# Two 3x3 convolutions in three steps: another order of the work on TensorE, ScalarE, VectorE and GpSimd

## What is computed

```python
def _conv(x, w):
    return lax.conv_general_dilated(x, w, window_strides=(1, 1), padding='SAME', ...)
for _ in range(N_STEPS):                       # 3 steps, H_STEP = 1/3
    t = jax.nn.relu(_conv(x, w1) + b1[None, :, None, None])
    x = x + H_STEP * (_conv(t, w2) + b2[None, :, None, None])
return jax.nn.relu(x)
```

## Time and profile before

| | |
|---|---|
| median of 3 runs | 1165.74 us (1165.06 to 1167.67) |
| the profiled execution | 1166.12 us, its span 1164.3 us |
| PE busy | 1078.2 us, 93% |
| DVE busy | 1060.3 us, 91% |
| ACT busy | 653.4 us, 56% |
| POOL busy | 525.9 us, 45% |

### The profile page before, as it was taken

How to read it: one execution, slowest core, us unless ns; L and a number is a source line. 1 busy time by engine, 2 the same in 40 slices (tenths; PEclk the granted TensorE clock), 3 DMA queues, 4 the chain that set the end, 5 groups by cost and what they waited for, 6 DMA issues and landing times. The chain is left out here.

```text
span 1164.3 us, 20990 instructions
## 1 busy us (share of the span) xinstructions
PE 1078.2 (93%) x7238; PEld 604.7 (52%) x7238; DVE 1060.3 (91%) x1481; ACT 653.4 (56%) x1525; POOL 525.9 (45%) x416
## 2 busy tenths in 40 slices
PE   3279999999999999999969999999999999999995
PEld 3167777777777777777633333333333333333331
DVE  5459999999999999999958999999999999999995
ACT  4558888888888888988613232332234232342332
POOL 5134555444554555545323444534435445444440
PEclk9989999999999999999989999999999999999998
DMA  8101111111111111110000000210003000120003
GB/s 304 53 20 28 37 38 29 38 29 37 35 32 29 37 37 33 34 28 20 20 10 1 1 1 1 46 28 1 1 1 73 1 1 1 29 45 1 1 1 73
DMA packets 87544, 35.83 MB, mean 31 GB/s; under 512 B 70209, under 2 KB 86850, under 8 KB 86930
## 3 DMA queue, kind: packets, MB, share of 16 engines
q1 hardware_dynamic: 85634, 33.81, 11.0%
q0 software_dynamic: 768, 0.33, 0.1%
q10 hardware_dynamic: 1040, 0.35, 0.1%
HBM read 26.09 MB, written 8.39 MB: 30 GB/s over the span
## 5 line engine op out<-in xcount | busy, mean ns | idle before, releaser
L1082 PE MATMUL acc<-mixed,cwp 128*128 128x512 f32 x768 | 354.4, 607 | 5.1 <-DVE mixed L1143 2.9
L1082 PEld LDWEIGHTS acc<-mixed,cwp 128*128 128x128 f32 x768 | 139.7, 191 | 218.6 <-issue 214.8
L1100 ACT ACTIVATE y<-acc,cols 128x1024 f32<-128x1024 f32 x96 | 111.6, 1207 | 249.4 <-PE acc L1092 249.4
L1092 PE MATMUL acc<-mixed,cwp 64*64 64x512 f32 x1536 | 184.2, 600 | 11.7 <-POOL mixed L1143 11.5
L842 POOL TENSOR_TENSOR rstd<-var,half 128x8 f32<-128x8 f32 x32 | 80.9, 2527 | 217.6 <-DVE var L733 217.6
L522 DVE TENSOR_TENSOR prod<-qkv 128x1024 f32<-128x1024 f32 x128 | 155.6, 1219 | 7.6 <-POOL qkv L738 7.3
L532 DVE TENSOR_TENSOR prod<-attn,qkv 128x1024 f32<-128x1024 f32 x128 | 155.0, 1235 | 1.1
L1142 POOL TENSOR_TENSOR mixed<-xs 128x256 f32<-128x256 f32 x92 | 83.1, 903 | 156.7 <-DVE xs L1131 156.7
L564 PE MATMUL cb<-consts,prod 128*128 128x128 f32 x1024 | 135.8, 283 | 0.0
L1108 DVE TENSOR_TENSOR y<-y,acc 128x512 f32<-128x512 f32 x192 | 120.5, 678 | 15.9 <-ACT y L1100 15.9
L1116 DVE TENSOR_TENSOR y<-y,acc 128x512 f32<-128x512 f32 x192 | 123.0, 682 | 7.2 <-PE acc L1092 5.2
(11 more groups left out here) (172 smaller groups left out, 1550.1 us busy)
## 6 DMA issues: line engine op xcount, KB each, us to landing
xs<-in_x SPq DMA_DIRECT2D x4, 2048.0 KB, 16.6
xa<-in_x SPq DMA_DIRECT2D x32, 256.0 KB, 2.8
xr<-in_x SPq DMA_DIRECT2D x64, 128.0 KB, 2.9
out_y<-xs SPq DMA_DIRECT2D x32, 256.0 KB, 4.7
cw<-in_L_conv_w POOLq DMA_DIRECT2D x2, 144.0 KB, 4.2
consts<-in_consts ACTq DMA_DIRECT2D x1, 192.0 KB
group<-in_consts SPq DMA_DIRECT2D x1, 64.0 KB
w1n<-in_L_conv_w ACTq DMA_DIRECT2D x1, 64.0 KB
```

Source lines behind the costliest of these rows:

```text
L1082: pe.matmul(psum[PSUM_PAIR[v, q, j]][i][:, :, :], weights(v, i, j).rearrange("p n o -> p (n o)"), mixed[v][i][:, s0:s0 + WIDE, j, :], star ...
L1092: m = pe.matmul(psum[PSUM_PAIR[v, q, j]][i][out, :, :], edge_weights(v, i, j)[rows, :], mixed[v][i][rows, s0 + near:s0 + near + WIDE, j, : ...
L1100: act.activation(pairs(y[i][q][:, :, :]), m1, ACT.Identity, bias=cols[:, (6, 8)[v]:(7, 9)[v]]).then_inc(m1_out[i][q], 1)
```

## The change

It replaces the written order of all four engines by another one with the same pieces. The same pieces stand on the same engines: per iteration DVE makes the 8 outer pieces of x, the 8 outer and 4 inner pieces of h, POOL 8 inner pieces of x and 4 of h. No instruction is added or removed. The iteration's boundaries in the lists lie elsewhere (parts of step g - 1 and g - 2 are now written in round g), which alone changes nothing in the order. The table of PSUM pairs is changed with it. The pieces before the first iteration are as they were.

```diff
         PSUM_PAIR = {
-            (0, 0, 0): 2, (0, 0, 1): 3, (0, 0, 2): 0, (0, 0, 3): 1, (0, 1, 0): 2, (0, 1, 1): 3, (0, 1, 2): 0,
-            (0, 1, 3): 1, (1, 0, 0): 3, (1, 0, 1): 2, (1, 0, 2): 1, (1, 0, 3): 0, (1, 1, 0): 2, (1, 1, 1): 3,
+            (0, 0, 0): 3, (0, 0, 1): 2, (0, 0, 2): 0, (0, 0, 3): 1, (0, 1, 0): 3, (0, 1, 1): 2, (0, 1, 2): 0,
+            (0, 1, 3): 1, (1, 0, 0): 3, (1, 0, 1): 2, (1, 0, 2): 0, (1, 0, 3): 1, (1, 1, 0): 2, (1, 1, 1): 3,
             (1, 1, 2): 0, (1, 1, 3): 1
         }
...
         def dve_iteration(dve, g, steps):
+            if steps[1]:
...
+                dve_sums(dve, g - 1, 1, 0, 1)
+                dve_sums(dve, g - 1, 1, 1, 1)
+                mix_x(dve, g - 1, 0, 1, outer)
+                dve_y(dve, g - 1, 1, 0, 1, 0)
+                dve_y(dve, g - 1, 1, 0, 1, 1)
+                dve_x(dve, g - 1, 0, 1)
+                dve_y(dve, g - 1, 1, 1, 1, 0)
+                dve_y(dve, g - 1, 1, 1, 1, 1)
+                dve_x(dve, g - 1, 1, 1)
...
         def act_iteration(act, g, steps):
...
             if steps[0]:
+                act_m1(act, g, 0, 1, 0)
                 act_m1(act, g, 0, 0, 0)
...
+            if steps[1]:
+                act_result(act, g - 1, 0, 0)
+                act_result(act, g - 1, 1, 0)
+                act_result(act, g - 1, 0, 1)
+                act_result(act, g - 1, 1, 1)
...
-            for g in range(COUNT + 2 - 1):
-                iteration(eng, g, [0 <= g - s < COUNT for s in range(2)])
+            for g in range(COUNT + 3 - 1):
+                iteration(eng, g, [0 <= g - s < COUNT for s in range(3)])
```

More of the change, by code:

```diff
@@ L1204, in pe_iteration @@
[L1204 to L1214, removed]
@@ L1226, in pe_iteration @@
[L1226 to L1229, removed]
-        def act_iteration(act, g, steps):
+        def act_iteration(act, g, steps):
+            if steps[1]:
+                act_hidden(act, g - 1, 0, 1)
+                act_hidden(act, g - 1, 0, 0)
+                act_hidden(act, g - 1, 1, 1)
+                act_hidden(act, g - 1, 1, 0)
+                act_m1(act, g - 1, 0, 0, 1)
+                act_m1(act, g - 1, 0, 1, 1)
+                act_hidden(act, g - 1, 1, 3)
+                act_hidden(act, g - 1, 1, 2)
+                act_hidden(act, g - 1, 0, 2)
+                act_hidden(act, g - 1, 0, 3)
+                act_m1(act, g - 1, 1, 0, 0)
+                act_m1(act, g - 1, 1, 1, 0)
+                act_m1(act, g - 1, 1, 0, 1)
+                act_m1(act, g - 1, 1, 1, 1)
@@ new lines, in dve_iteration @@
+        def dve_iteration(dve, g, steps):
+            if steps[1]:
+                mix_h(dve, g - 1, 0, 0, inner)
+                dve_sums(dve, g - 1, 0, 0, 1)
+                mix_h(dve, g - 1, 1, 0, outer)
+                dve_sums(dve, g - 1, 0, 1, 1)
+                dve_y(dve, g - 1, 0, 1, 1, 1)
+                dve_y(dve, g - 1, 0, 1, 1, 0)
+                dve_y(dve, g - 1, 0, 0, 1, 1)
+                mix_h(dve, g - 1, 1, 1, outer)
+                dve_y(dve, g - 1, 0, 0, 1, 0)
+                mix_h(dve, g - 1, 1, 3, outer)
+                mix_h(dve, g - 1, 0, 2, inner)
+                mix_h(dve, g - 1, 0, 2, outer)
+                mix_h(dve, g - 1, 1, 2, outer)
+                mix_h(dve, g - 1, 0, 3, outer)
+                mix_h(dve, g - 1, 0, 3, inner)
+                dve_sums(dve, g - 1, 1, 0, 0)
+                dve_sums(dve, g - 1, 1, 1, 0)
+                dve_y(dve, g - 1, 1, 0, 0, 1)
+                dve_y(dve, g - 1, 1, 0, 0, 0)
+                dve_x(dve, g - 1, 0, 0)
+                dve_y(dve, g - 1, 1, 1, 0, 0)
+                dve_y(dve, g - 1, 1, 1, 0, 1)
+                mix_x(dve, g - 1, 0, 0, outer)
+                dve_x(dve, g - 1, 1, 0)
+                mix_x(dve, g - 1, 1, 0, outer)
+                mix_x(dve, g - 1, 1, 1, outer)
+                dve_sums(dve, g - 1, 1, 0, 1)
[7 more added lines that the diff above has]
+                dve_x(dve, g - 1, 1, 1)
+                mix_x(dve, g - 1, 1, 2, outer)
+                mix_x(dve, g - 1, 0, 3, outer)
+                mix_x(dve, g - 1, 1, 3, outer)
+                mix_x(dve, g - 1, 0, 2, outer)
+            if steps[0]:
+                dve_sums(dve, g, 0, 1, 0)
@@ new lines, in pool_iteration @@
+        def pool_iteration(pool, g, steps):
+            if steps[2]:
+                mix_x(pool, g - 2, 1, 2, inner)
+                mix_x(pool, g - 2, 0, 3, inner)
+                mix_x(pool, g - 2, 1, 3, inner)
+            if steps[1]:
+                mix_h(pool, g - 1, 1, 1, inner)
+                mix_h(pool, g - 1, 1, 0, inner)
+                mix_h(pool, g - 1, 1, 2, inner)
+                mix_h(pool, g - 1, 1, 3, inner)
+                mix_x(pool, g - 1, 0, 0, inner)
+                mix_x(pool, g - 1, 1, 0, inner)
+                mix_x(pool, g - 1, 1, 1, inner)
+                mix_x(pool, g - 1, 0, 1, inner)
+                mix_x(pool, g - 1, 0, 2, inner)
```

137 lines of the change are left out of this document (39 added, 98 removed).

## The result

| | before | after |
|---|---|---|
| median | 1165.28 us (5 runs, 1164.95 to 1167.67) | 1152.32 us (5 runs, 1151.02 to 1153.23) |
| span of the profiled execution | 1164.3 us | 1149.2 us |
| PE busy | 93% | 94% |
| DVE busy | 1060.3 us | 1044.5 us |

The ratio is 0.9885, with a 95% interval of 0.9874 to 0.9895: 1.15% faster. The forecast was 1154.3 us (ratio 0.990), the range 1152.0 to 1159.5. The time lies just inside the range's low end, and the gain is larger than forecast by more than its interval.

A forecast was written before the change was run, and what follows sets the result against it. PE was taken to bound the convolutions, with one avoidable wait per iteration. Terms -12.2 + 1.5 - 0.75 = -11.45 us took the median of 1165.74 us to 1154.3 us, range 1152 to 1159.5.

The forecast's parts named there:

- What bounds the kernel: Convolutions: PE bounds them, and its 1.11 us wait per iteration between 16 products and the edges is all order can return.
- the floor of 43.71 us: Convolution iteration on PE: its length without the wait behind the 16 products, against 44.82 us before.
- The end of the step: Last products and additions of each iteration: finishing image 0 first removes PE's wait of 1.11 us, 11 times, 12.2 us less.
- R: In each iteration, the moment when PE starts the 16 products that open a step; other times are counted from it.
- The term of 12.2 us: Wait of PE behind the 16 products: 1.11 us saved in each of 11 iterations by finishing image 0 first.
- The 0.17 us to spare: Behind the 16 products: image 1's chunk 2 lets PE go on at R + 6.90, the products last until R + 7.07.
- The hidden layer: Second convolution's first edges, waiting for DVE's inner piece of image 0's chunk 2: some 0.3 us to spare, cost 0.
- The slower rival: Second convolution's first edges: DVE's inner piece of chunk 2 comes late, PE waits 12 times, about 1172 us; chance 0.06.
- The last relus: ACT where a pair of images ends: four relus delay h by 1.37 us, costing 0.5 three times, 1.5 us more.
- The end: Behind the kernel's last edges: image 0's relu runs under image 1's work, so the last store starts 0.75 us earlier.
- The two engines' sharing: POOL and DVE: a POOL instruction beside an outer piece and an addition beside POOL are each held up by about 0.44 us.
- the small waits: Rival: POOL and DVE hold-ups bring back 0.26 to 0.31 us of PE's wait eleven times, 1157.7 us; chance 0.15.

The follow-up runs named there:

- The end alone: Kernel before with only the last pieces of a step reordered on DVE and POOL, image 0 finished first, then image 1: 1161.00 us, ratio 0.9957.
- the middle alone: Kernel before with only DVE's first-half additions and outer pieces of x, and POOL's inner pieces of that half, reordered in the second convolution: 1153.94 us, ratio 0.9893.
- that order alone: Kernel before with image 0 finished first in the very last step only: 1164.20 us, ratio 0.9986.
- the run with the collision: Changed kernel with two neighbours exchanged in POOL's list, image 0's chunk 3 before image 1's chunk 2: 1160.24 us, ratio 0.9948.

## Why the prediction was right or wrong

- **What bounds the kernel: right.** PE bounds the steps, and only the wait between products and edges could be given back. PE now has next to no wait there, and the floor of 43.71 us, worked out from groups of 8 and 12, is what the kernels with the new middle and the old end show.
- **The end of the step: the size right, the cause wrong.** The step that failed is "Now image 0 is finished first. With the same pair of edges ahead, DVE can take the first product ... from R - 0.65": it took for granted that DVE is free at that time. The kernel before reaches these products at R + 0.47, and the prediction's own rows show it, R + 0.47 being the first of the earlier trace rows. What frees DVE is the middle of the second convolution, of which the prediction's change part by part says nothing. The end alone takes away 0.22 of 1.11 us per step, the middle alone all of it. The times R + 1.0 and R + 4.75 came out because both had been changed; that the size of this term was right is luck as far as the cause that it names goes. The term of 12.2 us measured 11.9 (11.66 and the 0.24 of the relus below). The 0.17 us to spare were not there: POOL's two instructions end at R + 6.98 and not at R + 6.85, and PE starts 0.14 behind them and not 0.05, so that 0.05 us per step are lost.
- **The hidden layer: right.** PE does not wait at it in any step of the changed kernel: DVE's piece is done at 726.58 and PE starts at 727.05, 0.47 us to spare where 0.3 was forecast. The slower rival, which needed 1.25 us of delay there, did not come.
- **The last relus: mis-sized.** +1.5 us measured +0.2 by the steps and nothing by the runs. h came 0.87 us later and not 1.37: ACT is free for 2.76 us there in the changed kernel, not 2.63, and the four relus take 3.79 us from the first's start to the next instruction (754.18 to 757.97), not 4.0. The step lost 0.08 of the 0.87; DVE and PE had the rest in hand.
- **The end: mis-sized.** -0.75 us measured -2.64 in the profiled executions (-2.36 with that order alone). The relu's part was right (8.40 to 7.72 us from the last edges to its end). The step "Transfers are otherwise as before" failed: the stores of image 0 fill a gap in which nothing was transferred.
- **The two engines' sharing.** The hold-up of 0.43 per meeting was right: 1.21 or 1.23 against 1.63 to 1.66 for an addition, with and without POOL. In the run with the collision the addition starts at 706.33, when POOL's instruction has 0.55 us left, and loses 0.40; POOL's next starts at 706.84, when the addition has 1.12 left, and loses 0.98. So each waits for what the other has left, less some 0.15 us. With the Trainium skill's rule that the first to start has the pair for the whole instruction (SBUF — State Buffer, Who interferes with whom) the trace agrees to within these 0.15. The prediction's working of the small waits, in which each of POOL's two instructions would come to 1.29, is not borne out: they take 1.12 and 1.06, and the wait came back at 0.05 and not at 0.31 us.
- The sum was -11.45 us, of which -10.7 for the steps with their relus (-12.2 + 1.5), where -11.66 came, and -0.75 for the end. With the measured terms it is -11.66 - 2.64 = -14.3 in the profiled executions and -13.0 between the medians. The relus (1.3 us) and the end (1.9 us) were both missed on the same side.

## What to carry to other kernels

Where a wait ends at an engine's last piece, follow that engine back to where it fell behind, and not just over the last few rows: here 1.85 us per step were lost on DVE 8 to 15 us ahead of the wait, in meetings with an engine that is 45% busy. A wait that gets shorter can come up again elsewhere: the end alone cut it from 1.05 to 0.53 us and gave back only 0.22, so compare the length of the step. Before costing a new order, check that each engine is free at the time from which the sum counts. And read the transfers in slices at the end of a kernel: here a gap in them was worth more than the last computation.

## What was not expected of the hardware

Behind a wait of PE of 2.48 us the granted clock fell in 8 of 11 steps, to 0.68 in the 5.35 us behind it in the step shown, and cost up to another 1.70 us; in the other 3 steps it stayed at 1.00 behind the same wait. Waits of 1.05 us and less cost only themselves in every step. How the clock behaves between these lengths was not tried.
